# The last, half-filled row chunk of the experts' down product goes through TensorE with all 128 rows

## The reference, cut to what matters

```
scores = xt @ Wg.T                                  # 8 experts
topk_scores, topk_idx = top_k(scores, 2)
gate = silu(einsum('td,ehd->teh', xt, W1))          # H = 704
up   = einsum('td,ehd->teh', xt, W2)
y    = einsum('teh,edh->ted', gate * up, W3)        # the down product
out  = einsum('te,ted->td', w, y)                   # w: the top two scores
```

## Time and profile before

| | |
|---|---|
| median of 3 runs | 1150.21 us |
| lowest, highest | 1147.30, 1152.08 us |
| span of the profiled execution, first to last instruction | 1151.0 us |
| PE busy | 928.8 us, 81% |
| DVE, POOL, ACT busy | 669.2, 590.9, 445.6 us |
| part with the experts' tiles | about 822 to 1118 us of the span |

### The profile page before, as it was taken

The page is one execution under the profiler, slowest core; times in us unless marked ns, Lnnn a source line. Parts: engine busy times, 40 slices in busy tenths (PEclk is TensorE's granted clock), DMA queues, the critical chain, the costliest instruction groups (busy, mean ns, idle before and its releaser), DMA issues. The chain is left out here.

```text
span 1151.0 us, 16215 instructions
## 1 busy us (share of the span) xinstructions
PE 928.8 (81%) x5148; PEld 731.9 (64%) x5149; DVE 669.2 (58%) x1097; ACT 445.6 (39%) x827; POOL 590.9 (51%) x481
## 2 busy tenths in 40 slices
PE   5767677889877889885989877992699999999970
PEld 2344345457666546665657765672689899999970
DVE  4189777697457788547677872416634343443443
ACT  2455754355544445635345530322222222222210
POOL 2176675755446565546576743110578553335505
PEclk9869877899886899996899987995699999999995
DMA  9440030000044000026000040004365312311304
GB/s 322 161 175 1 1 111 37 1 15 1 1 163 132 1 9 7 1 75 220 1 8 8 1 147 1 15 1 169 123 207 127 125 48 100 112 36 36 109 19 146
DMA packets 48954, 85.44 MB, mean 74 GB/s; under 512 B 6292, under 2 KB 38696, under 8 KB 46856
## 3 DMA queue, kind: packets, MB, share of 16 engines
q1 hardware_dynamic: 43032, 65.77, 17.0%
q0 software_dynamic: 5872, 19.02, 5.7%
HBM read 65.64 MB, written 14.55 MB: 70 GB/s over the span
## 5 line engine op out<-in xcount | busy, mean ns | idle before, releaser
L373 POOL TENSOR_TENSOR u<-dtx,b_all 128x512 f32<-128x512 f32 x256 | 326.6, 1288 | 212.9 <-DVE h L620 209.7
L620 DVE TENSOR_TENSOR_SCAN h<-da,u 128x512 f32<-128x512 f32 x256 | 308.6, 1217 | 136.8 <-ACT da L455 89.5
L455 ACT ACTIVATE da<-dt_,a_neg 128x512 f32<-128x512 f32 x256 | 174.8, 689 | 133.3 <-DVE h L620 132.5
L746 PE MATMUL ysum<-ident,h 128*128 128x128 f32 x1024 | 159.3, 301 | 57.9 <-DVE h L620 44.5
L746 PEld LDWEIGHTS ysum<-ident,h 128*128 128x128 f32 x1024 | 132.5, 156 | 104.2 <-DVE h L620 56.8
L924 PE MATMUL pv<-pT,ctx_n 128*128 128x128 f32 (+1 forms) x832 | 109.5, 288 | 7.6 <-DVE x_all L681 7.6
L924 PEld LDWEIGHTS pv<-pT,ctx_n 128*128 128x128 f32 (+1 forms) x832 | 104.6, 204 | 10.8 <-DVE x_all L681 9.1
L895 PE MATMUL pa<-ctx_t,xnT_a 128*128 128x401 f32 (+1 forms) x256 | 97.3, 508 | 13.9 <-DVE sim L602 12.6
L1367 DVE TENSOR_TENSOR hid<-act_,ps_u 128x352 f32<-128x352 f32 x78 | 40.6, 521 | 86.8 <-ACT act_ L1221 86.8
L1221 ACT ACTIVATE act_<-ps_g 128x352 f32<-128x352 f32 x78 | 36.3, 466 | 104.2 <-PE ps_u L1478 104.2
L1503 PE MATMUL ps_y<-w_hi,hidT_hi 128*128 x234 | 70.9, 303 | 2.7 <-DVE hidT_lo L1381 2.7
(11 more groups left out here) (216 smaller groups left out, 1780.5 us busy)
## 6 DMA issues: line engine op xcount, KB each, us to landing
b_all<-b_dram SPq DMA_DIRECT2D x16, 1024.0 KB, 4.6
ctx_t<-in_ctxT SPq DMA_DIRECT2D x4, 1601.0 KB
ctx_n<-in_ctx SPq DMA_DIRECT2D x4, 1536.0 KB
ffn_sorted<-yg SPq DMA_DIRECT2D x1, 4992.0 KB, 22.5
ffn_sorted<-y_sb SPq DMA_DIRECT2D x39, 128.0 KB
tok_in<-tok SPq DMA_DIRECT2D x35, 128.0 KB, 2.0
mask<-in_mask SPq DMA_DIRECT2D x16, 200.1 KB, 2.4
w_raw<-in_w1T SPq DMA_DIRECT2D x4, 704.0 KB, 4.2
```

Source lines behind the costliest of these rows:

```text
L373: nc.gpsimd.tensor_tensor(u[:, i % 2, :], dtx[:, j % 2, :], b_all[:, n, :], ALU.mult).then_inc(u_ok, 1)
L455: nc.scalar.activation(da[i % DS][:], dt_[:, j % 2, :], ACT.Exp, scale=a_neg[:, j, n:n + 1]).then_inc(da_ok, 1)
L620: nc.vector.tensor_tensor_scan(h[:, i % HS, :], da[i % DS][:], u[:, i % 2, :], 0.0, ALU.mult, ALU.add).then_inc(scan_ok, 1)
L746: last = nc.tensor.matmul(ysum[:, t * P:(t + 1) * P], h[:, i % HS, t * P:(t + 1) * P], ident[:], is_transpose=True, start=n == 0 and t == ...
```

## The change

Both `hidT` tensors get their upper 64 rows of the sixth chunk cleared once, by two copies on VectorE from the cleared part of `w_raw`, after a wait for the memset. The matmuls of the sixth chunk then take all 128 rows of both operands; rows 64 to 127 are zero on both sides. TensorE waits once for the clearing before its first tile.

```
                 nc.vector.memset(w_raw[H_LAST:P, :, NW - D:NW], 0.0).then_inc(w_pad, 1)
+                dve.wait_ge(w_pad, 1)
+                for part in (hidT_hi, hidT_lo):
+                    nc.vector.tensor_copy(part[H_LAST:P, KH - 1, :], w_raw[H_LAST:P, 0, NW - D:NW - D + P]).then_inc(w_pad, 1)
                 dve.wait_ge(iota_ok, 2)
...
                     for c in range(KH):
-                        rows_in = P if c < KH - 1 else H_LAST
                         for n, (x, w) in enumerate(parts):
-                            last = nc.tensor.matmul(ps_y[:, 0:D], x[0:rows_in, c, :],
-                                                    w[0:rows_in, at(e % 2 * NW + (2 * NGU + c * D), D)],
+                            last = nc.tensor.matmul(ps_y[:, 0:D], x[:, c, :],
+                                                    w[:, at(e % 2 * NW + (2 * NGU + c * D), D)],
                                                     start=c == 0 and n == 0, stop=c == KH - 1 and n == 2)
                     last.then_inc(y_mm, 1)
 
+                pe.wait_ge(w_pad, 3)
                 transpose_tokens(0, 0)
```

## The result

The changed kernel takes 1137.45 us (median of 4 runs, 1136.38 to 1139.13), the kernel before 1150.91 (4 runs). The ratio is 0.9883, 95% interval 0.9859 to 0.9908: 1.2% faster, 13.5 us. The forecast was 1138.4. The profiled execution has a span of 1137.3 us, against 1151.0.

A forecast was written before the change was run, and what follows sets the result against it. The prediction took TensorE, busy 155.62 of 156 us among the experts' tiles, as the bound. Its terms, -7.8 - 4.9 + 0.4 + 0.5 = -11.8 us, gave a median of 1138.4 us, range 1133.5 to 1145.

The forecast's parts named there:

- The bubble is at the change of the row count: In each tile's TensorE work, the missing 0.33 us lies around the 64-row matmuls, where weight loads are not drawn ahead.
- Rows cost nothing: In down's sixth chunk, a matmul at pace takes 0.12 us with 128 rows as with 64.
- The way in: From 128-row to 64-row matmuls in down: the whole 0.20 us a tile goes, 39 x 0.20 = 7.8 us.
- The way out: From down's last matmuls to the transposes: 0 to 0.13 us a tile goes; taken as 4.9 us gained.
- The two copies: Clearing copies on VectorE's chain between memset and first small operation: 0.4 us lost, between 0.3 and 0.54.
- The waits for tokens: tok_in loads at weight reloads land as before, TensorE waits 0.33 us at one or two: 0.5 us lost.
- Rival 2: Token loads fall clear of the reloads, the 3.7 us stall goes too: 1134.7 us; chance 0.12.
- the forecast case: Whole kernel: tile period becomes 6.86 us, median 1138.4 us, own range 1135.5 to 1141.5; chance 0.65.
- The sum: Whole kernel: -7.8 - 4.9 + 0.4 + 0.5 = -11.8 us, giving a median of 1138.4 us.
- Rival 3: At the sixth chunk nothing comes free, only the copies' cost is left: 1150.6 us; chance 0.05.
- rival 4: At the tok_in wait behind each of six reloads, the faster loop outruns token loads: 1156.9 us, slower; chance 0.04.

The follow-up runs named there:

- experiment 1: Kernel before, with the 64-row chunk first in each down product instead of last: 1157.22 us, ratio 1.0060.
- experiment 2: Kernel before, with a tile's three 64-row matmuls set apart, one behind each of the first three 128-row chunks: 1179.61 us, ratio 1.0253.
- 4: Changed kernel, with only the very last matmul of each down product back at 64 rows: 1154.35 us, ratio 1.0031.
- 3: Changed kernel, with 96 rows instead of 128 in the sixth chunk's matmuls: 1137.25 us, ratio 0.9882.
- the two profiles on the third chip: Both kernels run again unaltered on another chip: changed kernel 1181.82 us, ratio 0.9880; kernel before 1196.86 us.
- experiments 7: Kernel before, with each tok_in load issued as soon as its buffer is free, ahead of the store, on a second chip: 1191.84 us, ratio 0.9969.
- 8: Changed kernel, with each tok_in load issued as soon as its buffer is free, ahead of the store, on a second chip: 1181.60 us, ratio 0.9879.

## Why the prediction was right, point by point

- **The bubble is at the change of the row count.** Right. Taking it away took the steps of 0.21 and 0.23 out of every tile; experiments 1, 2 and 4 moved, multiplied and restored it (0.82 us for four more changes in experiment 2, 0.31 to 0.34 for the two in 4 and 1), and 3 showed that it belongs to 64 rows and not to 96.
- **Rows cost nothing.** Right: 128, 96 and 64 rows all go at 0.12.
- **The way in, 0.20 a tile.** Right.
- **The way out, 0.13 a tile, taken between 0 and 0.13.** Right as a mechanism: the transposes follow at 0.12, also in experiment 1. In size the tile gained 7.187 - 6.893 = 0.294, and not 0.33. Every second tile of the loop is 6.92 to 6.93 and the others 6.86. In the longer ones the first weight load of `gate_up` starts 0.30 behind the pair of loads before it and in the others 0.22. Weight loads in order of time:

```profile
1002.16 0.25 PEld L1468 LDWEIGHTS ps_x<-ident,tok_in 128*128 128x128 f32 x2
1002.46 0.19 PEld L1481 LDWEIGHTS ps_g<-w_hi,tokT_hi 128*128 128x128 f32 x1
...
1009.09 0.25 PEld L1468 LDWEIGHTS ps_x<-ident,tok_in 128*128 128x128 f32 x2
1009.31 0.19 PEld L1481 LDWEIGHTS ps_g<-w_hi,tokT_hi 128*128 128x128 f32 x1
```

- **The two copies, 0.4.** Right: 0.41 on VectorE, and 0.37 to 0.43 on the experts' start.
- **The waits for tokens, 0.5 lost.** Wrong in sign. This is the step that failed: I let them land as before and TensorE wait for what it had saved. That held at the first one, before the loop's pace is reached: the third tile's `down` starts 854.06 - 789.93 = 64.13 behind the memset, and before it was 852.61 - 789.11 = 63.50. The copies explain 0.4 of that; the two shorter tiles gained nothing there and 0.2 to 0.3 more went, 0.9 us against the sum over 39 tiles. Behind it the later waits nearly went. The tiles from the earlier trace rows, at 18.08 for two, became ordinary, and the longest is now 7.54, between these rows of the chain:

```profile
943.65 2.15 PE ps_y L1505 x18
951.19 2.16 PE ps_y L1505 x18
```

  The first trace before has 0.3, 3.7 and 1.24 us of such waits behind the third tile, 5.2 in all; the first trace after has 0.9. That is 4.3 us gained in these two executions, 2.4 between the two profiles on the third chip, and 4 by experiments 7 and 8. Rival 2 had the mechanism: its working moved the load 0.66 us forward against the reload, from 1.12 behind it to 0.46, and the rows show 0.6 to 1.0 us, to about 0.2 behind. It came together with the forecast case, and the load did not have to be in front of the whole reload for it.
- **The sum.** Forecast -11.8. Measured: -11.5 + 0.4 + 0.9, less 2.4 to 4.3 for the later waits, or -12.6 to -14.5. The first two traces close with it: from the memset to the last tile's `down` it is 1114.36 - 789.11 = 325.25 before and 1100.71 - 789.93 = 310.78 after, 14.5 less (the spans differ by 13.7, as the memset came 0.8 later in the second). The medians say -13.5, and their interval runs from -10.6 to -16.2, so it does not tell the forecast from the corrected sum; the traces do. The tile was off by 1.2 us one way and the waits by 2 to 4 the other. That these partly cancel is luck, and the forecast is nearer than its working deserved.
- **Rival 3** (nothing comes free) and **rival 4** (slower by waits) are out. Late loads of tokens do cost this kernel several us, but not as rival 4 had it: it let a shorter period leave them too little time. Experiments 1 and 4 have tiles 0.01 to 0.04 us longer than before and 2.4 and 3.6 us more of such waits behind the third tile, the changed kernel has 4.3 less, and experiment 2, with the longest period, again less than the kernel before. So neither a shorter nor a longer period is the rule; where the load falls among the parts of the reload fits which traces have the long waits, though not the size of each.

## What to carry to other kernels

A TensorE that is busy all the time can still have bubbles: look at distances between starts and at whether each weight load starts ahead of its matmul, above all where the number of rows falls to 64 or comes back. If the rest of the array would be idle anyway, cleared rows up to the full height (or to 96) cost nothing per matmul; grouping the low ones helps as well, since the price is per change. And when a loop's pace shifts, look at where its transfers fall against the others: here a fifth to a third of the gain came from loads that were issued 0.6 to 1.0 us earlier against a reload.

## What the runs showed of the hardware that was not expected

- 96 of 128 rows flow like 128; a single 64-row matmul among seventeen of 128 rows costs a tile 7.20 - 6.89 = 0.31 us, as much as three in a row.
- The same program takes 1150 us on one chip and 1195 on two others, and two stalls of ScalarE account for it, marked as released from elsewhere: two tiles take 45.7 us at the first and 30.3 at the second (experiment 7), where the first chip has about 17 and 14. The ratio of the two kernels was 0.988 in the first comparison and on the third chip.
- A small load that the changed kernel issued ahead of the second of a reload's large parts landed after 5.0 to 5.4 us; behind that part, in the kernel before and experiments 1 and 2, it took 5.3 to 7.4, with 2.0 us as the usual time. A shift of 0.6 us between two queues' issues can so decide whether the engine that waits loses 1 to 4 us.
